# Two transformer blocks on one Trainium2 core: the attention's context product made in quarters of the array

## The reference, cut to what matters

```python
x = x + xattn0(layernorm(x), ctx_512)      # ctx_512: (16, 64, 64)
x = x + ffn0(layernorm(x))                 # 8 experts, the best 2 of each token
x = x + xattn1(layernorm(x), ctx_512)
x = x + ffn1(layernorm(x))
# xattn:
scores = einsum('bhsr,bhlr->bhsl', q_r, k_r)
attn = softmax(scores, axis=-1)
ctx_c = einsum('bhsl,bld->bhsd', attn, kv_rope)
ctx_lat = einsum('bhsd,hkd->bshk', ctx_c, w_kc_kv)
out = ctx_lat.reshape(b, s, H * K) @ Wo.T
```

## Time and profile before

| | us |
|---|---|
| median of 3 executions | 609.87 (604.2 to 611.73) |
| the profiled execution's own time | 609.28 |
| its span in the trace | 607.4 |
| attention loop of layer 0 in the trace | about 80 to 147 |
| attention loop of layer 1 in the trace | about 438 to 504 |

### The profile page before, as it was taken

One profiled execution on the slowest core, in us unless ns is written; L12 is line 12 of the kernel. 1 busy time (PEld: TensorE's weight loads), 2 busy tenths in 40 slices (PEclk: granted clock), 3 DMA queues, 4 the chain that ended last, 5 costly groups with the idle time before them and its releaser, 6 DMA issues.

```text
span 607.4 us, 7951 instructions
## 1 busy us (share of the span) xinstructions
PE 524.0 (86%) x2738; PEld 382.9 (63%) x2738; DVE 365.3 (60%) x865; ACT 153.1 (25%) x299; POOL 214.0 (35%) x198
## 2 busy tenths in 40 slices
PE   4798999998599999998878989999999984698970
PEld 4686867876256665665865656666677853476750
DVE  3442497885423333332849996778578887377654
ACT  3112243322222222221430111111244430243420
POOL 2100123320313333212105654475446760545540
PEclk9659999999599999999999999999999997699995
DMA  8910079340111711100700000000090000212216
GB/s 283 306 58 1 2 311 431 152 165 18 35 34 45 287 45 52 36 26 37 277 1 0 1 0 1 0 2 0 12 411 20 9 19 17 80 53 78 79 54 216
DMA packets 17160, 55.43 MB, mean 91 GB/s; under 512 B 2912, under 2 KB 10592, under 8 KB 15584
## 3 DMA queue, kind: packets, MB, share of 16 engines
q1 hardware_dynamic: 13280, 44.41, 19.9%
q0 software_dynamic: 3840, 10.49, 5.4%
HBM read 46.50 MB, written 8.39 MB: 90 GB/s over the span
## 4 chain that ended last, share of the span: by engine, by line
PE 66%; DVE 18%; POOL 5%; DMA 4%; issue 3%; ACT 2%; SPq 1%; another core or an unknown queue 1%; DVEq 0%; POOLq 0%
PE PSD L706 12%; PE PSD L736 8%; PE PSD L578 7%; PE PSD L851 5%; PE PSD L416 4%; PE PSD L420 4%; PE PSD L422 4%; PE PSD L421 4%; PE PSD L507 3%; PE PSD L563 3%; DVE R L1450 3%; POOL R L1551 3%; DMA X<-in_x 2%; DVE X L1414 2%; PE PSD L451 2%
## 5 line engine op out<-in xcount | busy, mean ns | idle before, releaser
L1551 POOL TENSOR_TENSOR R<-R 128x512 f32<-128x512 f32 x48 | 62.2, 1324 | 61.6 <-DVE R L1450 61.6
L1450 DVE TENSOR_TENSOR R<-PSD,ropeq 128x512 f32<-128x512 f32 (+1 forms) x112 | 72.8, 683 | 14.9 <-PE PSD L422 13.1
L706 PE MATMUL PSD<-R 128*128 x160 | 74.3, 608 | 0.0
L1492 POOL TENSOR_TENSOR R<-R,sbm 128x1024 f32<-128x1024 f32 x16 | 30.4, 1902 | 109.2 <-DVE sbm L1125 109.2
L1523 POOL DMA_INDIRECT yd_dram<-R,dest_of x40 | 39.3, 983 | 72.7 <-DVE R L1366 69.7
L736 PE MATMUL PSD<-R 128*128 x240 | 59.7, 385 | 2.7 <-DVE R L1366 1.9
L578 PE MATMUL PSD<-B,R 128*128 128x256 f32 x256 | 57.9, 379 | 0.0
L578 PEld LDWEIGHTS PSD<-B,R 128*128 128x128 f32 x256 | 48.2, 190 | 10.6 <-issue 4.8
L706 PEld LDWEIGHTS PSD<-R 128*128 128x128 f32 x160 | 31.2, 197 | 31.0 <-issue 30.1
L1356 DVE SCALAR_TENSOR_TENSOR R<-R,PSD 128x512 f32<-128x512 f32 (+1 forms) x40 | 21.9, 548 | 46.1 <-ACT R L989 46.1
L851 PE MATMUL PSD<-R 128*128 128x512 f32 x96 | 44.6, 600 | 5.5 <-POOL R L1551 4.1
(11 more groups left out here) (161 smaller groups left out, 957.6 us busy)
## 6 DMA issues: line engine op xcount, KB each, us to landing
R<-in_w SPq DMA_DIRECT2D x2, 4096.0 KB, 17.2
R<-in_wo SPq DMA_DIRECT2D x2, 2048.0 KB, 26.3
R<-in_w SPq DMA_DIRECT2D x2, 2048.0 KB, 16.6
R<-yd_dram SPq DMA_DIRECT2D x16, 256.0 KB, 4.9
R<-in_g SPq DMA_DIRECT2D x8, 512.0 KB, 6.5
R<-in_wq SPq DMA_DIRECT2D x2, 1024.0 KB, 15.8
xn_dram<-XN SPq DMA_DIRECT2D x16, 128.0 KB, 1.7
R<-in_wq SPq DMA_DIRECT2D x1, 2048.0 KB
```

Of the source, the lines that this page charges most:

```text
L706: mm = e.matmul(bank[bk], XS0[g % 3][:, dc, :], columns(w1f, g, dc, n), start=(dc == 0), stop=(dc == DC - 1))
L1450: ins = e.tensor_tensor(v3((pr if part else ro)[to, dst, :]), v3(bank[3 * (n % 2) + src][rows]), bc(ropeq[rows, v, :], 8), ALU.mult)
L1551: ins = e.tensor_tensor(RO[n % 2][:, j, :], RO[n % 2][:, j, :], PR[n % 2][:, j, :], ALU.add)
```

## The change

A context product per sequence becomes two, one per head of the pair (`par`). Each uses the 64 rows of the array in which that head's keys lie, the 64 x 64 block of `VB` there, and 64 columns. The zeros of the block-diagonal matrix are no longer multiplied. For sequence 0 the output half is that of the rows (`par ^ 0`), for sequence 1 the other one (`par ^ 1`); rows of one half always write one bank, `bank[6 + par]`. So the four results of a tile lie in four quarters: (bank 6, lower), (bank 7, upper), (bank 6, upper), (bank 7, lower). Each must be copied by itself to its quarter of `CT`, two of them to the other half of the partitions. DVE copies the first. ACT copies the other three, except in tile 7, where DVE takes the fourth as well.

```diff
@@ pe_attention
             def context(i):
                 e.wait_ge(*etc[l, i])
+                if i == 0:
+                    e.wait_ge(*(sub[0, 1] if l == 0 else sub[1, 2]))
+                else:
+                    e.wait_ge(*ctcd[l, i - 1])
+                    e.wait_ge(*ctca[l, i - 1])
+                    if i >= 3:
+                        e.wait_ge(*lgr[l, i - 3])
+                    if i >= 4:
+                        e.wait_ge(*rsr[l, i - 4])
                 for b2 in range(2):
-                    if i == 0:
-                        e.wait_ge(*(sub[0, 1] if l == 0 else sub[1, 2]))
-                    else:
-                        e.wait_ge(*(ctca if b2 else ctcd)[l, i - 1])
-                        if b2 == 0 and i >= 3:
-                            e.wait_ge(*lgr[l, i - 3])
-                        if b2 == 1 and i >= 4:
-                            e.wait_ge(*rsr[l, i - 4])
-                    e.matmul(bank[6 + b2], VB[:, 2 * i + b2, :], ET[i % 2][:, :, b2 * S:(b2 + 1) * S],
-                             start=True, stop=True).then_inc(*cmm.step((l, i, b2)))
+                    for par in range(2):
+                        rows, cols = SIDE[par], SIDE[par ^ b2]
+                        mm = e.matmul(bank[6 + par][cols], VB[rows, 2 * i + b2, rows], ET[i % 2][rows, :, b2 * S:(b2 + 1) * S],
+                                      start=True, stop=True)
+                        if b2 == 1:
+                            mm.then_inc(*cmm.step((l, i, par)))
@@ router
                 if j + 2 < TT:
                     e.wait_ge(*ctcd[l, j + 2])
+                    e.wait_ge(*ctca[l, j + 2])
@@ act_attention
                 if i < TT:
-                    e.wait_ge(*cmm[l, i, 1])
+                    e.wait_ge(*cmm[l, i, 0])
                     if i >= 2:
                         e.wait_ge(*prj[l, i - 2])
-                    e.copy(CT[i % 2][:, :, S:2 * S], bank[7].rearrange("p (a b) -> p a b", b=S)).then_inc(*ctca.step((l, i)))
+                    e.copy(CT[i % 2][LO, :, S:2 * S], v3(bank[6][HI]))
+                    e.wait_ge(*cmm[l, i, 1])
+                    ins = e.copy(CT[i % 2][HI, :, 0:S], v3(bank[7][HI]))
+                    if i < TT - 1:
+                        ins = e.copy(CT[i % 2][HI, :, S:2 * S], v3(bank[7][LO]))
+                    ins.then_inc(*ctca.step((l, i)))
@@ dve_attention
-                    e.tensor_copy(CT[i % 2][:, :, 0:S], bank[6].rearrange("p (a b) -> p a b", b=S)
-                                  ).then_inc(*ctcd.step((l, i)))
+                    ins = e.tensor_copy(CT[i % 2][LO, :, 0:S], v3(bank[6][LO]))
+                    if i == TT - 1:
+                        e.wait_ge(*cmm[l, i, 1])
+                        ins = e.tensor_copy(CT[i % 2][HI, :, S:2 * S], v3(bank[7][LO]))
+                    ins.then_inc(*ctcd.step((l, i)))
```

More of the change, by code:

```diff
@@ L43 @@
 ALLP, LO, HI = slice(0, P), slice(0, 64), slice(64, P)
+SIDE = (LO, HI)
 ROPE = ((0, ALLP, 0, 0, 0, ALLP), (0, ALLP, 3, 1, 2, ALLP), (2, ALLP, 1, 1, 0, ALLP), (2, ALLP, 2, 0, 2, ALLP),
```

## The result

| | before | after |
|---|---|---|
| median of the executions, us | 608.09 (604.2 to 611.73, 4) | 616.53 (613.79 to 621.04, 4) |
| ratio after to before | | 1.017, 95% interval 1.0119 to 1.0221 |
| profiled execution, its span | 609.28, 607.4 | 615.89, 614.0 |
| context of one tile, iteration 2 of layer 0 | 1.72 | 1.02 |
| attention loop of layer 0, first context to last projection | 64.53 | 72.22 |

Where the executions of a kernel fall in two groups, as those of `x_best_g1` further down do (598 to 604 and 607 to 609.3 us, six each), its ratio to the kernel before is that of the faster group alone, while every median is of all executions.

What follows compares the result with a forecast made beforehand. TensorE's context products led the chain, with DVE nearly as full and setting the pace in iterations 3 and 4. The profiled 609.28 us plus 2.5 (layer 0) and 0.6 (layer 1) gave 612.4, stated as 612.5, range 606 to 620.

Steps and rivals of the forecast that it cites:

- what bounds the kernel: Attention loop: TensorE without a gap, context 1.72 of 8.70 us a turn; DVE sets the pace in iterations 3 and 4.
- rivals 1 and 2: Context products: records begin in program order (621 us, chance 0.09), or quarters do not overlap at all (641 us, 0.04).
- rival 1: Context products: records begin in program order, eight taking 2.40 us, 0.68 more than before; 621 us, chance 0.09.
- Rival 3: Router's wait does not bind, so all 16 contexts save 0.61 to 0.86 us; 598 us, chance 0.05.
- the ring: Mid-loop wait chain from DVE through ACT's copies, router and scores back to DVE: 9.01 us against 8.70 before.
- the copies' spacing: ACT's context copies start 0.46 us apart back to back, so two more delay the last by 0.92 us.
- 9.01 against 9.24: Layer 0, iteration 3: forecast turn against the turn before, so DVE's delay drops from +0.62 to +0.39 us.
- the sum for layer 0: Delays followed through iterations 0 to 7 of layer 0's attention loop: it ends 2.5 us later.
- Iteration 7: ... +2.54: Layer 0, iteration 7: router released after two copies at 145.20 against 142.66, so 2.54 us later.
- half a microsecond: Start of layer 1: may begin that much earlier if each context saves 0.86 us; +1.3 in all.
- What is lost or won ahead of that meets the same point: End of layer 1: POOL's two low-part steps and DVE's L1240 end together at 496.85; tile 7 behind adds about +0.6.
- the upper bound: Layer 1's loss: at most +2.5 us, as layer 0; +0.6 taken, lower bound 0.

Runs made afterwards that it cites:

- x_best_g1: Changed kernel with the edits of x_order and x_tail, and layer 1's expert-weight pieces converted earlier: 605.53 us, ratio 0.9914 to the kernel before.
- x_fill: Changed kernel with unread filler products on TensorE ahead of the router in iterations 6 and 7: 610.51 us, ratio 1.0082 to the kernel before.
- x_copies: Changed kernel with the two full context products of before, its four copies and router wait kept: 619.66 us, ratio 1.0236 to the kernel before.
- a_again: The changed kernel once more, unchanged: 616.61 us, ratio 1.0166 to the kernel before.
- x_order: Changed kernel with two of ACT's three copies ahead of the exponential in iterations 0 to 5: 611.67 us, ratio 1.0071 to the kernel before.
- x_tail: Changed kernel with the last tiles' router and rank results in banks 4 and 5: 611.02 us, ratio 1.0088 to the kernel before.
- x_best: Changed kernel with the edits of x_order and x_tail together: 608.23 us, ratio 1.0028 to the kernel before.

## Why the prediction was right or wrong

**Right: what bounds the kernel, and the direction.** The quarters overlap fourfold. The context took 1.02 us where I had 1.11, and rivals 1 and 2 (2.40 and 3.69 us) are out. Had the eight records started in the order of the products, both of one product ahead of both of the next, they would have taken at least five places of 0.43, 2.15 us; four of them began at once at 96.21. The prediction hung rival 1 on the rule that matmuls start and end strictly in program order ("TensorE: Matmul & The Clock Gate", section Part 3: Packing small matmuls, of the Trainium skill). I had applied that rule to the two records of each product. The trace is at odds with that reading, and not with the rule taken product by product. Rival 3, that the saving shows, is out but for the start of layer 1: in iterations 2 to 7 the router waits for ACT's last copy. The page "TensorEngine Tiling (Array Packing)", section Performance Considerations, of the Trainium skill agrees with the trace: the emptying of PSUM became the limit, with copies of 64 partitions at 0.58 us.

**Right, 0.2 us off: the ring.** The forecast was 9.01 us, the turns are 9.22 to 9.27. By its terms, in iteration 2: 2.52 to the exponential (2.51 forecast), 1.34 to the first context copy (1.22), 1.91 through the three copies to the router (1.57), 0.44 to the transposes (0.70), 1.00 and 2.01 as forecast. The mis-sized term is the copies' spacing, 0.60 instead of 0.46, 0.28 us in all; the others nearly cancel. With the ring at 9.22 no turn of DVE is left that could take back what an earlier one lost, as I had reckoned for 9.01 against 9.24.

**Wrong: the sum for layer 0,** 2.5 us forecast and 7.69 measured. By stage of the prediction:

| stretch of layer 0 | forecast | measured |
|---|---|---|
| iteration 0, context to projection of tile 0 | +0.31 | +0.64 |
| to DVE's step of iteration 2 | 0 | +0.10 |
| the three turns to iteration 5 | +0.11 | +0.82 |
| to the transposes of iteration 5's turn (L514, now L515) | +0.98 | +1.24 |
| to the router of iteration 6 | +0.80 | +1.33 |
| to the router of iteration 7 | +0.34 | +3.77 |
| to the last projection | -0.04 | -0.21 |
| sum | +2.5 | +7.69 |

The first five rows are forecast at 2.2 and measured at 4.1; the copies' spacing is in all of them but the small second one. The step that failed is "Iteration 7: ... +2.54". It took TensorE's work behind the router at full clock. Transposes to projection took 1.73 us instead of 0.90, the projection 5.54 instead of 3.46 to the next step, router to transposes 0.90 instead of 0.70. Together that is 3.1 of the 3.77. x_fill shows that this is the clock: with TensorE busy during the same wait it is full, and the iteration takes 8.16 us, 3.2 less, and 0.2 from the 7.62 + 0.34 = 7.96 of the forecast. I had worked out a router released 1.84 us after the copy of `XN` (it was 138.22 - 135.91 = 2.31), and had not asked what an idle stretch of that length does to the clock.

**Wrong: layer 1,** 0.6 us forecast, 3.99 measured, of which -1.38 is the start (the prediction had "half a microsecond" there, and only in its range) and 5.37 the rest. The step that failed is "What is lost or won ahead of that meets the same point". The point is not fixed. POOL's pair follows ACT's conversion, which stands behind the three copies, so the pair moved with the loss:

```profile
501.44 4.66 POOL L1514 TENSOR_TENSOR g_lo<-R,g_hi 128x1024 fp32r<-128x1024 f32 x2 [1.38 <-ACT g_hi L966]
```

It ends at 506.10, while the projection at half clock still runs (503.08 to 508.49): POOL hides behind the loss here, and not the loss behind POOL. With the clock full, in x_fill, POOL's pair is what is left at that place, and takes back 1.5 of the 3.2 us. The router's wait of 2.34 us with the half clock behind it (499.9 to 506.7) is the same as in layer 0. I had named +2.5, layer 0's own figure, as the upper bound; with layer 0's 7.69 in its place the bound would have held.

**Right by luck: the total.** The range reached to 620 because of rival 1, which did not occur. It held the time because of that. The base helped too: I added 3.1 us to an execution of 609.28, 5.9 us of which lay in an expert stage that did not repeat, and in the later measurements the kernel before had medians of 605 to 606. So the loops were 8.6 us off and the total only 4.

## What to carry to other kernels

A smaller product can save nothing, or cost time, when its results need more instructions to be emptied: count the copies that follow and the waits that now hang on the last of them, and follow that chain round to the step that it began with before pricing the saving. Where a wait on TensorE grows (here from 0.46 to 2.34 us), add the work behind it at half the clock as a second case: it came to 3.1 us in layer 0. Of the six waits of 2.34 us in the traces here, one left the clock full. Results that share a bank with a slow reader can be moved to a bank that is free by then; here that was worth about 5 us in a layer. Copies moved ahead of an exponential that waits anyway were worth 3.4 us in layer 0, counted from the first context, and 0.4 in layer 1. Choose the stretch to compare with care: counted from the first projection, the loops hide nearly all that the shorter context saves.

## What the runs showed of the hardware that I had not expected

- Four 64 x 64 float32 products of 512 columns on four quarters, eight records of 0.43 us, took 1.02 us from the first to the next full product, 0.16 over a perfect fourfold overlap (after, iteration 2 of layer 0).
- A copy out of PSUM on ACT starts 0.46 us behind the one before it over all partitions, 0.49 where both read and write the same half (x_copies), and 0.59 to 0.60 where one side or both change their half (after, x_copies). The 0.58 us of each, at 512 elements a partition, does not change.
- The granted clock fell to 0.5 behind waits of TensorE, but not behind each. After 2.34 us it fell for 6.8 us (after in both layers, a_again in layer 1, x_order in layer 0) or for 3.4 (a_again in layer 0), and in layer 1 of x_order it did not. In x_copies the 2.23 us in iteration 6 of layer 0 left it at full, and it fell at 149.1, behind the 1.64 us of iteration 7; in layer 1 it fell behind both, for 3.4 us each. In iteration 1 x_fill and x_tail lost it behind a wait of 1.94 us, and after kept it behind 1.95. What decides between these is open; no run here was made for it.
- Beside POOL's two steps, together 4.66 us, a DVE step on two elements a partition took 2.33 us and one on 256 took 2.53 (x_best); the same two steps in after, with POOL idle, took 0.16 and 0.43 (506.73 and 506.92).
